# Attention and a mixture of experts on one core: 76 transfers a sequence in place of 103, with two experts' units interleaved on the partitions

## The chip, the core and the metric

The kernel runs on one core of one Trainium2 chip. The core has four compute engines: TensorE (PE, matrix products into PSUM banks), VectorE (DVE), ScalarE (ACT) and GpSimd (POOL). Each works through its own list of instructions in order and waits on semaphores for the others. A fifth, SyncE (SP), issues the transfers (DMAs); each raises a semaphore by 16 when it has landed. The metric is the device time of one execution in microseconds (us). Lower is better.

## What is computed

Sixteen sequences of 512 tokens with 128 channels pass one transformer layer in float32: causal attention with 16 heads of 64, a residual with layer norm, and a mixture of 32 experts of which 8 are chosen for each token.

```python
# attention, on h = layernorm(x)
q, k, v = (einsum('bsd,hde->bhse', h, W) for W in (Wq, Wk, Wv))
attn = softmax(where(causal, q @ k.T / sqrt(64), -inf))
y = h + concat_heads(attn @ v) @ Wo
x1 = x + layernorm(y, eps=1e-3) * gamma + beta
# experts, on h2 = layernorm(x1)
probs = softmax(h2 @ gate_w.T)                  # 32 experts
comb = top-8 of probs, divided by their sum, 0 elsewhere
for e in range(32):
    g, u = split(h2 @ gate_up_w[e].T)           # 64 each
    out += ((u * silu(g)) @ down_w[e].T) * comb[:, e]
result = x1 + out
```

## The kernel before

Everything of a sequence stays in SBUF. Products are made in float16 parts (`product`: high x high, high x low, low x high), so most tiles exist as a high half, written by ACT, and a low half, written by DVE or POOL. The four engines and SP have their orders written out by hand. The attention of sequence n, the experts of sequence n-1 (its last units, n-2) and the first steps of sequence n+1 are interleaved; a loop `for n in range(2, B - 2)` repeats one such list, and the first two and the last two sequences have lists of their own.

*Scores.* Projections give keys and queries of a pair of heads in `nat`. `place_qk(m, q)` (lines 303 to 312) copies them with six transfers, three for each head, 1 MB in all, to one of five slots of `score_ops`. The largest score of each row is found by DVE in a first, rough pass; POOL (`split_maxima`) scales it and splits it into high and low, PE turns it (`turn_maxima`), ACT copies the result to `rowmaxT` (`copy_maxima`), of 32 rows with 128 columns for a quad of four heads. `place_max(m, g)` (lines 314 to 321) puts these rows into two partitions of QB, so that the product subtracts them. Rows 16k to 16k+15 belong to pair k of the quad, eight for its high parts and eight for its low ones; there is one transfer for each eight. `scores` (line 457 on) waits for `placed[pair]` and, for each first head of a quad, for `max_placed`. ACT then takes exponentials (`exps`, L848) and the high half (`p_high`), POOL the low half (`p_low`, L1497), and PE multiplies by the values (`times_v`).

*Experts.* DVE makes the weights `comb` of 128 tokens x 4 chunks x 32 experts (`weigh`, L1210), PE turns them (`turn_weights`, L535), ACT copies them to `combT`, and `keep_weights(p)` (line 323) stores them as rows of the DRAM tensor `comb_rows`, one for an expert, with one transfer for each chunk. A unit j is a pair of experts, 64 partitions for each; `spread_weights(p, j)` (line 329, issues L335) reads its two rows of weights back and copies each to 64 partitions of `weighed(p, j)`, one of a ring of four buffers (`RING`), which is free when `unit_low(p, j-4)` is done. POOL multiplies the unit by it (`weigh_unit`, L1512), ACT takes the high half (`unit_high`), POOL the low half (`unit_low`, L1516), and PE multiplies by the down weights (`down_product`). In the last sequence each unit has a buffer of its own and DVE does the multiplication (`weigh_last`).

SP's list in the loop, with the order that matters below: 

```python
place_max(n, 3)
spread_weights(n - 1, 4); place_qk(n + 1, 0); spread_weights(n - 1, 5); spread_weights(n - 1, 6)
spread_weights(n - 1, 7); load_xb(n); place_qk(n + 1, 1); spread_weights(n - 1, 8)
spread_weights(n - 1, 9); place_qk(n + 1, 2); place_max(n + 1, 0); spread_weights(n - 1, 10)
```

PE's list in the loop comes to `scores(n + 1, 0, 0)`, which needs that `place_max(n + 1, 0)`, after `up_product(n - 1, 9)` and the projections of pair 3, and to `times_v(n + 1, 0)` some ten microseconds behind. A sequence has 103 transfers: 48 of keys and queries, 16 of maxima, 4 stores and 32 spreads of weights, two loads of x and one store of the result.

Of the kernel before, what the change touches and what calls it, by code (L numbers as in the profile page):

```python
# [53 lines left out]
def layer(nc, x, wq, wk, wv, wo, gamma, beta, gate, gate_up, down, ident_c, mask_c,  # L54
          key_rows_c, query_rows_c, tail_c, out):
    with ExitStack() as ctx:
# [14 lines left out]
        def slot_of(m, q):  # L71
# [60 lines left out]
        a_hi, a_lo = halves[:, 0], halves[:, 1]  # L132
        logits, dropped, shifted, ex, comb = (
            sb(name, [P, C, NE], F32) for name in ("logits", "dropped", "shifted", "ex", "comb"))
        top8 = sb("top8", [P, C, TOPK], F32)
# [140 lines left out]
        def _(sp):  # L276
# [37 lines left out]
            def place_max(m, g):  # L314
                wait(sp, score_mm, UNITS * 2 * (m * PAIRS + 2 * g + 1 - SLOTS + 1))
                sp.wait_ge(rowmaxT_ready, m * QUADS + g + 1)
                for k in range(2):
                    home = QB[E:E + MAX_ROWS, slot_of(m, 2 * g + k)].rearrange("a b (c p) -> a (b c) p", c=C)
                    for part in range(2):
                        at = 16 * k + 8 * part  # L320
                        sp.dma_start(home[part:part + 1], rowmaxT[at:at + 8, :]).then_inc(max_placed[g], 16)  # L321

            def keep_weights(p):
                sp.wait_ge(combT_ready, p + 1)
                wait(sp, a32_done, p * EP)
                for c in range(C):
                    sp.dma_start(comb_rows[:, c * P:c * P + P], combT[c * NE:c * NE + NE, :]).then_inc(comb_stored, 16)

            def spread_weights(p, j):
                if j == 0:  # L330
                    sp.wait_ge(comb_stored, 16 * C * (p + 1))
                if p < B - 1:
                    wait(sp, a_lo_done, p * EP + j - RING + 1)
                for e in range(2):
                    sp.dma_start(weighed(p, j)[ED * e:ED * e + ED, :],  # L335
                                 comb_rows[2 * j + e:2 * j + e + 1, :].to_broadcast([ED, S])).then_inc(spread_sem(p, j), 16)

# [49 lines left out]
        def _(pe):  # L387
# [73 lines left out]
            def scores(m, h, u):  # L461
                pair, ab, b = h // 2, h % 2, score_bank(h, u)
                slot = slot_of(m, pair)
                take(b, exp_done, m * H * UNITS + h * UNITS + u + 1)
                if m == 0 and h == 0 and u == 0:
                    pe.wait_ge(rows_loaded, 80)
                    pe.wait_ge(rows_filled, 4)
                if u == 0 and ab == 0:
                    pe.wait_ge(placed[pair], 96 * (m + 1))
                    if h % 4 == 0:  # L470
                        pe.wait_ge(max_placed[h // 4], 64 * (m + 1))
                for t in ((0,), (1, 3), (2,))[u]:
                    cols, at = S - t * P, (384 if t == 3 else 0)
                    dst = bank[b][:, at:at + cols]
                    keys = slice(t * P, t * P + P)
                    mm(dst, KA[:, slot, ab, keys], QA[:, slot, ab, t * P:S], True, False, True)
                    if t == 0:
                        mm(dst[:, P - 4:P], tail[:, 0:P], tail[:, P:P + 4], False, False, True)
                    n = BARRED_BY[t]
                    for side, first, end in ((KB0, 2 * n, cols), (KB1, 0, n), (KB2, n, 2 * n)):  # L480
                        last = mm(dst[:, first:end], side[:, slot, ab, keys], QB[:, slot, ab, t * P + first:t * P + end], False, True, True)
                last.then_inc(score_mm, 1)
# [49 lines left out]
            def turn_weights(m):  # L532
                take(XB, combT_ready, m + 1)
                pe.wait_ge(comb_done, m + 1)
                pe.transpose(bank[XB][:, 0:P], comb[:, :, :].rearrange("p c e -> p (c e)"), ident32[:, :]).then_inc(combT_mm, 1)  # L535

# [247 lines left out]
        def _(act):  # L784
# [53 lines left out]
            def copy_maxima(m, g, b):  # L838
                act.wait_ge(rowmaxT_mm, m * QUADS + g + 1)
                wait(act, max_placed[(g - 1) % QUADS], 64 * (m + 1) if g else 64 * m)  # L840
                copy(rowmaxT[:, :], bank[b][0:8 * C, 0:P]).then_inc(rowmaxT_ready, 1)
# [185 lines left out]
        def _(dve):  # L1027
# [170 lines left out]
            def weigh(p):  # L1198
# [10 lines left out]
                wait(dve, combT_mm, p)  # L1209
                dve.tensor_tensor(comb[:, :, :], exm[:, :, :], exinv[:, :].rearrange("p (c a) -> p c a", a=1).to_broadcast([P, C, NE]),  # L1210
                                  ALU.mult).then_inc(comb_done, 1)
# [15 lines left out]
            def weigh_last(p, j):  # L1227
                dve.wait_ge(su_done, p * EP + j + 1)
                dve.wait_ge(last_spread[j], 32)
                dve.tensor_tensor(weighed(p, j), weighed(p, j), unit(p, j), ALU.mult).then_inc(last_weighed, 1)  # L1230
# [232 lines left out]
        def _(pool):  # L1463
# [45 lines left out]
            def weigh_unit(p, j):  # L1509
                pool.wait_ge(su_done, p * EP + j + 1)  # L1510
                pool.wait_ge(comb_spread[j % RING], 32 * (p * (EP // RING) + j // RING + 1))
                pool.tensor_tensor(weighed(p, j), weighed(p, j), unit(p, j), ALU.mult).then_inc(a32_done, 1)  # L1512
# [119 lines left out]
```

## Time and profile before

| | |
|---|---|
| three timed runs, median | 1753.68 us |
| lowest, highest | 1750.7, 1754.48 us |
| the profiled execution, its own time | 1747.59 us |
| its span, first to last instruction | 1745.7 us |
| mean granted TensorE clock in it | 0.991 of full |
| busy: PE, DVE, ACT, POOL | 1633.9, 1462.4, 1404.4, 1403.9 us |

In the rows of the profile, L389 is the line of the helper that issues all ordinary matrix products, and L786 that of the helper for ACT's copies, so operations are told apart by the tiles that they write and read. SPq stands for SP's queue: the time of a row there is that of issuing transfers, not of moving data. A row of the timeline gives start, duration, engine, line, operation, output and inputs, and how many were merged (x4); brackets give the idle time ahead of it and what ended that. Everything is in microseconds, and times of the timeline count from the span's start.

### The profile page before, as it was taken

What the parts mean: (1) busy time and instruction counts of PE and PEld (TensorE: products, weight loads), DVE (VectorE), ACT (ScalarE), POOL (GpSimd) and SP (SyncE); (2) the same over time, 40 slices, a digit from 0 to 9 for tenths busy, and PEclk for the clock granted to TensorE, in tenths of its full rate; (3) what the DMA queues carried; (4) which work ended last, traced back from release to release, by engine and by line L of the source; (5) the groups of instructions that cost most, each with busy time, mean ns of one, the idle gap of its engine ahead of it and who ended that gap; (6) DMA issues with size and microseconds to landing.
All of it is one profiled execution on the core that took longest, in us unless ns stands there. A gap on an engine that the chain in (4) does not pass through costs nothing.

```text
span 1745.7 us, 56980 instructions
## 1 busy us (share of the span) xinstructions
PE 1633.9 (94%) x21209; PEld 1113.7 (64%) x21209; DVE 1462.4 (84%) x4484; ACT 1404.4 (80%) x2364; POOL 1403.9 (80%) x1164
## 2 busy tenths in 40 slices
PE   3799999999999999999999999999999999999868
PEld 1366766666666666666666666666676666667655
DVE  7999889797887978879797887979889797887757
ACT  2799888797887879788797888879788787888752
POOL 4477997888879788887888979788897888889880
PEclk9999999999999999999999999999999999999999
DMA  5554554646455464544646454473645546435423
GB/s 181 128 122 106 145 136 123 166 106 158 104 132 129 106 178 110 142 115 115 174 106 159 110 140 124 104 186 95 158 117 133 139 106 165 123 109 138 112 79 105
DMA packets 219444, 226.26 MB, mean 130 GB/s; under 512 B 27041, under 2 KB 185249, under 8 KB 218913
## 3 DMA queue, kind: packets, MB, share of 16 engines
q1 hardware_dynamic: 219168, 222.61, 49.8%
q8 instruction: 170, 2.79, 0.7%
q14 instruction: 106, 0.86, 0.2%
HBM read 82.53 MB, written 5.24 MB: 50 GB/s over the span
## 4 chain that ended last, share of the span: by engine, by line
PE 61%; SPq 8%; DVE 8%; DMA 6%; POOL 6%; issue 5%; ACT 5%; POOLq 0%; ACTq 0%; DVEq 0%
PE bank_r L389 15%; PE bank_s L389 12%; PE bank_v L389 8%; PE bank_g L389 8%; PE bank_u L389 8%; PE bank_x L389 7%; SPq L321 3%; POOL p_lo L1497 2%; DMA expert_room<-comb_rows 2%; SPq L335 2%; SPq L311 1%; SPq L312 1%; POOL expert_room L1512 1%; DMA xt<-in_x 1%; SPq L310 1%
## 5 line engine op out<-in xcount | busy, mean ns | idle before, releaser
L1497 POOL TENSOR_TENSOR p_lo<-p,p_hi 128x1280 f16<-128x1280 f32 x256 | 674.7, 2636 | 149.0 <-ACT p_hi L786 148.2
L848 ACT ACTIVATE p<-bank_s,back 128x512 f32<-128x512 f32 (+1 forms) x768 | 461.4, 615 | 61.9 <-PE bank_s L389 53.8
L389 PE MATMUL bank_s<-score_ops 128*128 128x62 f16 (+10 forms) x4096 | 405.6, 233 | 20.6 <-DMA score_ops<-rowmaxT 15.3
L389 PEld LDWEIGHTS bank_s<-score_ops 128*128 128x128 f16 x4096 | 278.1, 97 | 192.5 <-issue 46.8
L1512 POOL TENSOR_TENSOR expert_room<-expert_room 128x512 f32<-128x512 f32 x240 | 304.4, 1275 | 34.7 <-DMA expert_room<-comb_rows 17.4
L786 ACT ACTIVATE p_hi<-p 128x1280 f16<-128x1280 f32 x256 | 324.6, 1268 | 7.8 <-PE bank_r L389 2.2
L1516 POOL TENSOR_TENSOR halves<-expert_room,halves 128x512 f16<-128x512 f32 x240 | 276.4, 1162 | 29.0 <-ACT halves L786 27.3
L1124 DVE CUSTOM_DVE_ANT_0 max_junk<-bank_r,mask 128x384 f16<-128x384 f32 (+3 forms) x523 | 232.1, 474 | 36.6 <-PE bank_g L389 16.3
L389 PE MATMUL bank_x<-w_hi,halves 128*128 128x128 f16 x1920 | 199.1, 220 | 2.0 <-POOL halves L1516 2.0
L786 ACT ACTIVATE halves<-expert_room 128x512 f16<-128x512 f32 x240 | 150.1, 625 | 44.8 <-POOL expert_room L1512 32.2
L389 PE MATMUL bank_x<-w_lo,halves 128*128 128x128 f16 x960 | 173.2, 220 | 0.0
L389 PEld LDWEIGHTS bank_x<-w_hi,halves 128*128 128x128 f16 x1920 | 155.2, 98 | 20.3 <-issue 6.2
L389 PE MATMUL bank_r<-nat 64*128 64x384 f16 (+3 forms) x523 | 106.1, 300 | 15.3 <-DVE o L1137 9.8
L1124 DVE CUSTOM_DVE_ANT_0 max_junk<-bank_u,mask 128x512 f16<-128x512 f32 (+3 forms) x202 | 99.0, 505 | 6.1 <-PE bank_g L389 4.0
L389 PE MATMUL bank_r<-tanh_room,w_hi 128*128 128x512 f16 x338 | 101.8, 383 | 0.5 <-DVE o L1137 0.4
L389 PEld LDWEIGHTS bank_x<-w_lo,halves 128*128 128x128 f16 x960 | 94.1, 98 | 7.3
L389 PE MATMUL bank_r<-v_hi,p_hi 128*128 128x65 f16 x870 | 87.9, 194 | 2.1 <-POOL p_lo L1497 1.4
L389 PE MATMUL bank_r<-v_hi,p_lo 128*128 128x65 f16 x870 | 87.9, 194 | 0.0
L389 PE MATMUL bank_r<-v_lo,p_hi 128*128 128x64 f16 x870 | 87.8, 192 | 0.0
L786 ACT ACTIVATE nat<-bank_r 128x512 f16<-128x512 f32 x110 | 65.9, 599 | 26.2 <-PE bank_r L389 24.1
L389 PE MATMUL bank_u<-tanh_room,w_hi 128*128 128x512 f16 x264 | 78.7, 380 | 7.5 <-DVE v_lo L1112 6.2
L1124 DVE DVE_READ_ACCUMULATOR2_ANT rowmax<- 128x1 f32 x1024 | 85.2, 83 | 0.1
(298 smaller groups left out, 5015.4 us busy)
## 6 DMA issues: line engine op xcount, KB each, us to landing
score_ops<-nat SPq DMA_DIRECT2D x256, 256.0 KB, 3.8
score_ops<-nat SPq DMA_DIRECT2D x512, 128.0 KB, 3.6
expert_room<-comb_rows SPq DMA_DIRECT2D x480, 128.0 KB, 3.0
xt<-in_x SPq DMA_DIRECT2D x16, 256.0 KB, 3.5
xb<-in_x SPq DMA_DIRECT2D x16, 256.0 KB, 4.1
score_ops<-rowmaxT SPq DMA_DIRECT2D x256, 2.0 KB
out_y<-expert_room SPq DMA_DIRECT2D x16, 256.0 KB, 3.4
score_ops<-comb_rows SPq DMA_DIRECT2D x32, 128.0 KB, 3.0
```

Source lines behind the costliest of these rows:

```text
L310: sp.dma_start(score_ops[0:E, 0:4, slot, ab, :], home[rows, K_HI:K_HI + 1].to_broadcast([E, 4, S])).then_inc(placed[q], 16)
L311: sp.dma_start(score_ops[0:E, 4:6, slot, ab, :], home[rows, Q_HI:Q_LO + 1]).then_inc(placed[q], 16)
L312: sp.dma_start(score_ops[E:P, 0:5:4, slot, ab, :], home[rows, K_LO:Q_HI + 1]).then_inc(placed[q], 16)
L321: sp.dma_start(home[part:part + 1], rowmaxT[at:at + 8, :]).then_inc(max_placed[g], 16)
L335: sp.dma_start(weighed(p, j)[ED * e:ED * e + ED, :], comb_rows[2 * j + e:2 * j + e + 1, :].to_broadcast([ED, S])).then_inc(spread_sem(p, j ...
L389: return pe.matmul(dst, lhsT, rhs, start=start, stop=stop, skip_group_check=shared)
L786: return act.activation(dst, src, ACT.Copy)
L848: act.activation(p32[:, h % P_SLOTS, at:at + cols], bank[score_bank(h, u)][:, 0:cols], ACT.Exp, scale=back[:, SC_SCORE:SC_SCORE + 1]).then ...
L1124: done = dve.tensor_tensor_reduce(max_junk[:, k % 2, at:at + cols], bank[b][:, at:at + cols], mask[:, S - cols:S], 1.0, NEG, ALU.add, ALU. ...
L1497: pool.tensor_tensor(p_lo[:, slot, :], p32[:, slot, :], p_hi[:, slot, :], ALU.subtract).then_inc(p_lo_done, 1)
L1512: pool.tensor_tensor(weighed(p, j), weighed(p, j), unit(p, j), ALU.mult).then_inc(a32_done, 1)
L1516: pool.tensor_tensor(a_lo[:, j % 2, :], weighed(p, j), a_hi[:, j % 2, :], ALU.subtract).then_inc(a_lo_done, 1)
```

## The change

Three kinds of transfer are merged, and the lists of all engines and their order stay.

- `place_max` issues one transfer for each pair of heads (16 rows to two partitions) in place of two (8 rows to one partition): 8 a sequence for 16.
- `keep_weights` issues one store for four. So that the rows of `combT` come out in the order of `comb_rows`, `comb` is laid out with the expert ahead of the chunk; DVE writes it through a rearranged view.
- `spread_weights` issues one transfer of 256 KB for two of 128 KB: 16 a sequence for 32. Its 128 partitions read two rows in turn, so even partitions hold the first expert of the unit and odd ones the second. The gate, up and down weights are interleaved on the host in the same way.

The counts in the waits on `max_placed`, `comb_stored` and the spreads' semaphores are halved or quartered to match. The number of bytes moved is the same.

```diff
-            sb(name, [P, C, NE], F32) for name in ("logits", "dropped", "shifted", "ex", "comb"))
+            sb(name, [P, C, NE], F32) for name in ("logits", "dropped", "shifted", "ex"))
+        comb = sb("comb", [P, NE, C], F32)
...
-                    for part in range(2):
-                        at = 16 * k + 8 * part
-                        sp.dma_start(home[part:part + 1], rowmaxT[at:at + 8, :]).then_inc(max_placed[g], 16)
+                    sp.dma_start(home, rowmaxT[16 * k:16 * k + 16, :]).then_inc(max_placed[g], 16)
...
-                for c in range(C):
-                    sp.dma_start(comb_rows[:, c * P:c * P + P], combT[c * NE:c * NE + NE, :]).then_inc(comb_stored, 16)
+                sp.dma_start(comb_rows.rearrange("e (c p) -> (e c) p", c=C), combT).then_inc(comb_stored, 16)
...
-                    sp.wait_ge(comb_stored, 16 * C * (p + 1))
+                    sp.wait_ge(comb_stored, 16 * (p + 1))
...
-                for e in range(2):
-                    sp.dma_start(weighed(p, j)[ED * e:ED * e + ED, :],
-                                 comb_rows[2 * j + e:2 * j + e + 1, :].to_broadcast([ED, S])).then_inc(spread_sem(p, j), 16)
+                sp.dma_start(weighed(p, j),
+                             comb_rows[2 * j:2 * j + 2].rearrange("a (b s) -> b a s", b=1).to_broadcast([ED, 2, S])).then_inc(spread_sem(p, j), 16)
...
-                        pe.wait_ge(max_placed[h // 4], 64 * (m + 1))
+                        pe.wait_ge(max_placed[h // 4], 32 * (m + 1))
...
-                pe.transpose(bank[XB][:, 0:P], comb[:, :, :].rearrange("p c e -> p (c e)"), ident32[:, :]).then_inc(combT_mm, 1)
+                pe.transpose(bank[XB][:, 0:P], comb[:, :, :].rearrange("p e c -> p (e c)"), ident32[:, :]).then_inc(combT_mm, 1)
...
-                dve.tensor_tensor(comb[:, :, :], exm[:, :, :], exinv[:, :].rearrange("p (c a) -> p c a", a=1).to_broadcast([P, C, NE]),
+                dve.tensor_tensor(comb[:, :, :].rearrange("p e c -> p c e"), exm[:, :, :], exinv[:, :].rearrange("p (c a) -> p c a", a=1).to_broadcast([P, C, NE]),
                                   ALU.mult).then_inc(comb_done, 1)
...
-    gu = gate_up_w.reshape(EP, 2, 2, ED, D).transpose(4, 0, 2, 1, 3)
+    gu = gate_up_w.reshape(EP, 2, 2, ED, D).transpose(4, 0, 2, 3, 1)
...
-        "down": cont(down_w.reshape(EP, 2, D, ED).transpose(1, 3, 0, 2).reshape(P, EP * D)),
+        "down": cont(down_w.reshape(EP, 2, D, ED).transpose(3, 1, 0, 2).reshape(P, EP * D)),
```

## Rows read from the trace of the kernel before

**Rows 1.** The page: span, busy time of PE, and packets of the DMA engines.

```profile
span 1745.7 us, 56980 instructions
PE 1633.9 (94%) x21209; PEld 1113.7 (64%) x21209; DVE 1462.4 (84%) x4484; ACT 1404.4 (80%) x2364; POOL 1403.9 (80%) x1164
DMA packets 219444, 226.26 MB, mean 130 GB/s; under 512 B 27041, under 2 KB 185249, under 8 KB 218913
```

**Rows 2.** Busy time by stretches: the sum of eight stretches of 103.3 us, 332.0 to 1157.7.

```profile
sum 826.40, PE 798.97 PEld 548.03 DVE 701.32 ACT 693.71 POOL 700.78; mean PE 99.87 PEld 68.50 DVE 87.67 ACT 86.71 POOL 87.60
```

**Rows 3.** List of waits, whole run: who waited, for whom, us, times, longest.

```profile
PE bank_s L389 <- DMA score_ops<-rowmaxT: 15.3, 13, 2.2
PE bank_r L389 <- DVE o L1137: 10.2, 13, 0.9
PE bank_x L535 <- DVE comb L1210: 4.4, 12, 0.4
PE bank_u L389 <- POOL p_lo L1497: 2.8, 2, 2.3
PE bank_x L389 <- POOL halves L1516: 2.0, 6, 0.8
...
POOL p_lo L1497 <- ACT p_hi L786: 148.2, 95, 3.5
...
POOL expert_room L1512 <- DMA expert_room<-comb_rows: 17.4, 16, 2.7
```

**Rows 4.** Chain of waits, 905 to 951.5: start, us, what.

```profile
930.40 4.13 DMA expert_room<-comb_rows
...
949.31 1.68 DMA score_ops<-rowmaxT
```

**Rows 5.** Timeline of ACT and of PE around 951.

```profile
943.52 0.27 ACT L786 ACTIVATE rowmaxT<-bank_v 32x128 f16<-32x128 f32 x1 [1.39 <-PE bank_v L389]
...
951.12 0.38 PE L389 MATMUL bank_s<-score_ops 128*128 128x512 f16 x1 [1.15 <-DMA score_ops<-rowmaxT]
```

**Rows 6.** Timeline of SP's issues, 920.5 to 952.

```profile
921.09 2.79 SPq L321 DMA_DIRECT2D score_ops<-rowmaxT  x4
...
929.75 4.60 SPq L335 DMA_DIRECT2D expert_room<-comb_rows  x6
...
942.10 0.63 SPq L310 DMA_DIRECT2D score_ops<-nat  x1
...
946.45 0.61 SPq L312 DMA_DIRECT2D score_ops<-nat  x1
947.15 2.79 SPq L321 DMA_DIRECT2D score_ops<-rowmaxT  x4
```

**Rows 7.** Issues by line (ns: shortest/median/longest), and time from issue to landing.

```profile
L335 SPq DMA_DIRECT2D expert_room<-comb_rows x480: 444/597/1612, 173.5 to 1683.6; - x160
DMA to landing us min/median/max: 2.7/3.0/5.5
...
L321 SPq DMA_DIRECT2D score_ops<-rowmaxT x256: 634/653/872, 53.7 to 1644.6; - x128
...
score_ops<-nat SPq DMA_DIRECT2D x256, 256.0 KB, 3.8
```

**Rows 8.** Timeline of POOL, 930 to 957.

```profile
929.04 1.17 POOL L1516 TENSOR_TENSOR halves<-expert_room,halves 128x512 f16<-128x512 f32 x1
930.76 2.62 POOL L1497 TENSOR_TENSOR p_lo<-p,p_hi 128x1280 f16<-128x1280 f32 x1 [0.56 <-ACT p_hi L786]
934.67 1.27 POOL L1512 TENSOR_TENSOR expert_room<-expert_room 128x512 f32<-128x512 f32 x1 [1.28 <-DMA expert_room<-comb_rows]
```

**Rows 9.** Busy time by stretches; last: PE's clock, DMA engines' share, GB/s.

```profile
939.40:947.10 7.70, 7.41 (x104) 5.48 (x105) 6.49 (x21) 5.44 (x10) 7.47 (x8) 1.00 1.01 230
```

**Rows 10.** The tile comb, 905 to 912: ns of its multiplication.

```profile
L1210 DVE TENSOR_TENSOR comb<-bank_x,exinv x1: 291/291/291, 905.8 to 905.8; 128x128 f32<-128x128 f32 x1
```

**Rows 11.** Timeline of PE at the same step of the next sequence.

```profile
1054.02 0.38 PE L389 MATMUL bank_s<-score_ops 128*128 128x512 f16 x1 [0.33 <-DMA score_ops<-rowmaxT]
```

More of the change, by code:

```diff
@@ L132, in layer @@
         a_hi, a_lo = halves[:, 0], halves[:, 1]
-        logits, dropped, shifted, ex, comb = (
-            sb(name, [P, C, NE], F32) for name in ("logits", "dropped", "shifted", "ex", "comb"))
+        logits, dropped, shifted, ex = (
+            sb(name, [P, C, NE], F32) for name in ("logits", "dropped", "shifted", "ex"))
+        comb = sb("comb", [P, NE, C], F32)
         top8 = sb("top8", [P, C, TOPK], F32)
@@ L839, in copy_maxima @@
                 act.wait_ge(rowmaxT_mm, m * QUADS + g + 1)
-                wait(act, max_placed[(g - 1) % QUADS], 64 * (m + 1) if g else 64 * m)
+                wait(act, max_placed[(g - 1) % QUADS], 32 * (m + 1) if g else 32 * m)
                 copy(rowmaxT[:, :], bank[b][0:8 * C, 0:P]).then_inc(rowmaxT_ready, 1)
@@ L1228, in weigh_last @@
                 dve.wait_ge(su_done, p * EP + j + 1)
-                dve.wait_ge(last_spread[j], 32)
+                dve.wait_ge(last_spread[j], 16)
                 dve.tensor_tensor(weighed(p, j), weighed(p, j), unit(p, j), ALU.mult).then_inc(last_weighed, 1)
@@ L1510, in weigh_unit @@
                 pool.wait_ge(su_done, p * EP + j + 1)
-                pool.wait_ge(comb_spread[j % RING], 32 * (p * (EP // RING) + j // RING + 1))
+                pool.wait_ge(comb_spread[j % RING], 16 * (p * (EP // RING) + j // RING + 1))
                 pool.tensor_tensor(weighed(p, j), weighed(p, j), unit(p, j), ALU.mult).then_inc(a32_done, 1)
```

## The prediction

> **What bounds the kernel now.** I read the page's busy shares first. PE is busy 94% of the span [rows 1]: PE sets the pace, and what can be won is its idle time. Cut into eight sequences of 103.3 us, the run shows PE busy 99.87 us in each [rows 2], so 3.4 us are idle. The list of waits says for what. PE's largest entry is the landing of the row maxima, 15.3 us in 13 waits, about one of 1.2 us in each looped sequence; the next of the loop is 10.2 us for DVE's o, which the change doesn't touch [rows 3]. POOL has 17.4 us in 16 waits for spread weights [rows 3].
>
> Why do the maxima land late? In the chain of waits the last thing before 951.0 us is their landing, 1.68 us from issue [rows 4], and PE, idle for 1.15 us, then starts the first score product of the next sequence [rows 5]. So the wait is for `place_max(n+1, 0)`. Its data were ready long before: ACT's copy to rowmaxT ended at 943.79 [rows 5]. What it waits for is the queue: on SP the last issue of `place_qk(n+1, 2)` ends at 947.06 and the maxima begin at 947.15 [rows 6].
>
> **The stretch replayed with the change.** SP pays about the same for every issue: 0.60 us for a spread of 128 KB, 0.65 for a maximum of 2 KB [rows 7], with 0.04 to 0.1 between two. I take these for the merged forms; the bounds are 0.44 and 1.61, the shortest and longest spread [rows 7]. I start at 921.09, which hangs on ACT's copy for quad 3 and so stays, and follow the list of SP.
> - From 921.09 to 929.75 SP issues four maxima (2.79 us), two halves of spread 4 and the six transfers of `place_qk(n+1, 0)` [rows 6]. Two maxima and one half fall away, 2 x 0.70 + 0.69 = 2.1 us, so spread 5 is issued at 927.6 and not in halves at 929.75 and 930.4.
> - The second half landed 4.13 us after its issue, at 934.53 [rows 4], and POOL, free since 933.38, waited 1.28 us for it [rows 8]. Merged it may take 3.0 us (the median of 128 KB) or 6.0 (twice that); nat's transfer, 256 KB too, has 3.8 [rows 7]. I take 4.1, near to the half's own 4.13 at this place: 931.7. POOL's wait is gone, with 1.7 us to spare; at 6.0 it would be 0.2.
> - Spread 6 ends at 928.8. Spread 7 needs `unit_low` 3, whose subtraction ends at 930.21 [rows 8]: here SP really waits, and is through at 930.9. xb follows (0.6), then `place_qk(n+1, 1)` with the 4.3 that the first took (the 8.66 us above less maxima and spread): 935.8. Spreads 8 and 9 need the next two subtractions, which POOL now reaches 1.28 us earlier, the second at 936.9: SP is through at 937.5. `place_qk(n+1, 2)` takes its 5.0 us (942.10 to 947.06 [rows 6]): 942.5.
> - `place_max(n+1, 0)` is then held by ACT's copy (943.79) and not by the queue: two issues, at 943.9 and 944.6, for four from 947.15.
>
> The landing: no row has sixteen rows of 256 B going to two partitions. It can't be sooner than a single part now, 1.68 us [rows 4]; above stands the nat transfer of 256 KB, 3.8 us [rows 7]. So it lands between 946.3 and 948.4, and PE asks for it at 949.97 [rows 5]: hidden at both ends, by 3.7 or 1.6 us. I take 1.7, since the data are those of the first row.
>
> How the rows are spread over engines is what a rule speaks against. The page counts 27041 packets under 512 B [rows 1]. If each of the 1648 transfers of the sixteen sequences ended in sixteen small packets that would be 26368, and the 2048 rows of maxima on top make 28416, too many by 1375; with eight for a maximum it is 26368 in all, and the first loads fill the rest. The Trainium skill, page "DMA: Bandwidth & Descriptors", section "Why a DMA increments its semaphore by 16 and not by 1", gives the reason: a transfer runs on the largest number of engines up to 16 that divides the slowest dimension of both sides. By that rule the trace's eight are right, a merged maximum (two partitions at the destination) runs on two engines with eight rows each, and the section "Rules for kernel authors" of the same page advises to keep all sixteen in use. The sum by that rule is the same: the maximum lands somewhere within the bounds above.
>
> Bandwidth could hold the queue too. From 939.4 to 947.1 the DMA engines are full, share 1.01 at 230 GB/s [rows 9]. The bytes don't change. Three `place_qk` of 1 MB, five spreads and xb of 256 KB are 4.7 million bytes, 20.5 us at 230 GB/s; begun at 923.3 (925.4 before) that ends at 943.8, again no later than ACT's copy. The engines allow it, just.
>
> **The sum**, against the profiled run: span 1745.7 us [rows 1], its own time 1747.6; the median of the three timed runs is 1753.7, 6.1 more.
> - PE's 13 waits for the maxima [rows 3], all removed: -15.3.
> - POOL's waits for spreads [rows 3] fall, but POOL is not the bound. PE waits 2.0 us for its halves and 2.8 for p_lo [rows 3], so 0 to -4.8; I take -1, since what POOL itself waits for is mostly ACT's p_hi, 148.2 us [rows 3].
> - The maxima of the other three quads, `place_qk` and the loads of x come earlier, and PE's list has no wait for any of them: 0. Their cover is PE's work on the heads before.
> - `keep_weights`, one issue for four, lands 1 to 1.5 us sooner; POOL's first weighed unit follows, inside the 17.4 us above: 0.
> - `comb` with experts outermost: DVE stores with a stride. It takes 0.29 us now [rows 10], and PE waits for it 4.4 us in 12 waits [rows 3]. A gain is excluded (as many elements, strided). At most I let it double: 0.29 x 16 = +4.6. I take 0, its own row. Weights are reordered on the host and their products keep their shapes: 0.
> - Given back: PE, 1.2 us early, meets what was next latest. In the sequence that ends at 1054 PE came late by itself, and the wait was only 0.33 us [rows 11]: the wait absorbs delays that would show otherwise. Bounds 0 and +7 (0.5 us in each of 14 sequences); I take 15% of the gain, +2.3, since POOL and SP advance at the same time.
> - The fill and the last sequence: no wait of PE for a DMA stands in the list there: 0. For the last, each spread has a buffer of its own.
>
> Together -15.3 - 1 + 2.3 = -14.0 us. Profiled 1733.6; in the median 1753.7 - 14.1 = 1739.6.
>
> **Rivals.**
> *Half of it.* The maxima are early, but PE meets ACT or POOL almost at once; 7 us stay, 1746.7. For it speaks the 0.33 us above; against, that POOL, too, loses its 1.28 us wait ahead of this place.
> *Nothing.* The change doesn't shorten the queue: a merged issue costs SP as much as its two parts, as there are as many rows to describe, and the maxima come when they come now. 1753.7. Against it: 2 KB and 128 KB cost nearly the same issue [rows 7].
> *More.* SP leaves the loop's chain altogether, and PE wins 1 us more of its remaining 2.2 us a sequence, in 13: 1726.
> *Slower.* The merged spread lands so late that the ring of four starves POOL. The places: spread 5 (issued 927.6, needed 933.4, 5.8 us) and spread 10, which follows `unit_low` 6 at about 949 and is weighed near 955.3, 6.2 us. It decides from a landing of 6 us, twice the 3.0 of a half. At 8 us POOL waits 2.2 + 1.8 us a sequence for 1.3 now, 2.7 more; less PE's 1.2 that is +1.5 x 13 = +20: 1773.7. Against it: no half took over 5.5 us [rows 7].
>
> **How the numbers follow.** Forecast (1732 to 1745) 0.55, more 0.10, half 0.15, nothing 0.12, slower 0.08. The predicted time is the forecast's, 1739.6. The range, 1726 to 1754, reaches from "more" to "nothing"; the slower case and the far ends are left out. Under 0.2% (3.5 us) a change can't be told from none here. Faster: forecast, more and nearly all of half, 0.78; same: nothing, with a little of half, 0.13; slower 0.09.
>
> **What the changed profile would show.** PE's entry for the DMA of rowmaxT gone, or under 2 us; POOL's for spreads under 6; SP waiting longer for ACT's rowmaxT and POOL's halves, as these now start its work; 128 maxima issues at 0.65 us, spreads at 0.60 and landing in 3.4 to 4.1; a sequence of 102.3 us. The prediction is wrong if merged issues take over 0.9 us, if PE's 15 us come back under ACT p or POOL p_lo, or if spreads land after 6 us.

## The result, and the profile after

The changed kernel takes 1711.3 us (median of four runs, 1710.19 to 1712.3) against 1752.19 for the kernel before (four runs, 1746.62 to 1754.48): 0.9771 of it, with a 95% interval of 0.9746 to 0.9796, 41 us less. In the profiled executions the span fell from 1745.7 to 1710.5 us, by 35.2.

The page after, its first lines, the packets, the shares of the chain that ended last, and one row of its DMA issues (instructions, KB each, median us from issue to landing):

```profile
span 1710.5 us, 56548 instructions
PE 1626.2 (95%) x21209; PEld 1111.5 (65%) x21209; DVE 1463.2 (86%) x4484; ACT 1400.7 (82%) x2364; POOL 1402.4 (82%) x1164
...
DMA packets 212783, 226.20 MB, mean 132 GB/s; under 512 B 20384, under 2 KB 178592, under 8 KB 212256
...
PE 82%; DVE 8%; POOL 4%; issue 4%; ACT 1%; DMA 0%; SPq 0%; POOLq 0%; DVEq 0%; ACTq 0%
...
expert_room<-comb_rows SPq DMA_DIRECT2D x240, 256.0 KB, 3.5
```

Before, the same line of the chain began with these shares:

```profile
PE 61%; SPq 8%; DVE 8%; DMA 6%; POOL 6%; issue 5%; ACT 5%; POOLq 0%; ACTq 0%; DVEq 0%
```

SP's queue and the DMAs, together 14% of the chain, are gone from it. PE's waits after (for whom, us, times, longest) have no entry for the maxima, where [rows 3] had 15.3 us in 13; of the two waits of the first row one is in the fill (11.8 us), the other behind the loop:

```profile
PE bank_r L386 <- DVE hT L1099: 13.0, 2, 11.8
PE bank_r L386 <- DVE o L1134: 10.0, 13, 0.9
...
PE bank_x L532 <- DVE comb L1207: 6.0, 13, 0.5
```

SP, on the other hand, waits more for its data. Its waits, before and then after:

```profile
SPq L307 <- DVE nat L1107: 180.7, 46, 20.5
SPq L316 <- ACT rowmaxT L786: 144.3, 34, 7.8
SPq L335 <- POOL halves L1516: 109.8, 72, 5.7
```

```profile
SPq L308 <- DVE nat L1104: 240.9, 60, 21.0
SPq L317 <- ACT rowmaxT L783: 211.2, 44, 10.1
SPq L332 <- POOL halves L1513: 205.2, 116, 8.0
```

**Where the time went.** PE turns `comb` once in each sequence, so two such rows tell how long a sequence takes. Timeline of PE before, one row a sequence:

```profile
906.22 0.30 PE L535 MATMUL bank_x<-ident,comb 128*128 128x128 f32 x1 [0.37 <-DVE comb L1210]
1009.55 0.30 PE L535 MATMUL bank_x<-ident,comb 128*128 128x128 f32 x1 [0.37 <-DVE comb L1210]
1113.94 0.30 PE L535 MATMUL bank_x<-ident,comb 128*128 128x128 f32 x1 [0.37 <-DVE comb L1210]
```

and after (481.34 and 582.68 are neighbours, and 278.67 and 1393.86 eleven sequences apart):

```profile
278.67 0.30 PE L532 MATMUL bank_x<-ident,comb 128*128 128x128 f32 x1 [0.46 <-DVE comb L1207]
481.34 0.30 PE L532 MATMUL bank_x<-ident,comb 128*128 128x128 f32 x1 [0.46 <-DVE comb L1207]
582.68 0.30 PE L532 MATMUL bank_x<-ident,comb 128*128 128x128 f32 x1 [0.47 <-DVE comb L1207]
...
1393.86 0.30 PE L532 MATMUL bank_x<-ident,comb 128*128 128x128 f32 x1 [0.46 <-DVE comb L1207]
```

Before, these sequences take 103.3 and 104.4 us; over ten of the loop, each measured from one PE instruction to the same one a sequence later, 102.8 to 106.9, 104.2 on average. After, they take 101.3 to 101.6: (1393.86 - 278.67) / 11 = 101.4. The ten give 28.4 of the 35.2 us, the sequences behind them and the tail 7.4; the fill ahead is 0.5 longer. I call that time of a sequence its period below.

### The profile page after: what moved, and what is told of

Same layout as the page of the kernel before. It is cut to its first block, busy times and chain, and to the rows that moved or that the text cites. A ratio compares the mean times of both kernels' runs of the same rounds, so it can differ in the third digit from the quotient of the medians.

```text
span 1710.5 us, 56548 instructions
## 1 busy us (share of the span) xinstructions
PE 1626.2 (95%) x21209; PEld 1111.5 (65%) x21209; DVE 1463.2 (86%) x4484; ACT 1400.7 (82%) x2364; POOL 1402.4 (82%) x1164
## 4 chain that ended last, share of the span: by engine, by line
PE 82%; DVE 8%; POOL 4%; issue 4%; ACT 1%; DMA 0%; SPq 0%; POOLq 0%; DVEq 0%; ACTq 0%
PE bank_r L386 20%; PE bank_s L386 15%; PE bank_v L386 11%; PE bank_u L386 11%; PE bank_g L386 10%; PE bank_x L386 10%; POOL p_lo L1494 2%; PE bank_r L395 2%; DVE max_junk L1121 1%; PE bank_v L395 1%; DVE stats L1028 1%; PE bank_x L395 1%; POOL halves L1513 1%; POOL expert_room L1509 1%; DVE x L1160 1%
## 5 line engine op out<-in xcount | busy, mean ns | idle before, releaser
L386 PE MATMUL bank_r<-tanh_room,w_hi 128*128 128x512 f16 x338 | 101.7, 383 | 0.5 <-DVE o L1134 0.4
L386 PEld LDWEIGHTS bank_r<-v_hi,p_hi 128*128 128x128 f16 x870 | 79.1, 98 | 6.1 <-issue 2.1
```

What stands on the lines that cost most here:

```text
L386: return pe.matmul(dst, lhsT, rhs, start=start, stop=stop, skip_group_check=shared)
```

## The experiments

Each kernel was timed beside the kernel before on the same chip; those medians were 1748.12 us (e1 to e4), 1749.9 (e5, e6, e10 and e11) and 1750.41 (the two e9, e12 and e14). The two e9 kernels have two runs each, the others four to ten. The table holds what each gave; "period" is the mean of ten looped sequences in the profiled execution, and the last two columns are PE's waits for the maxima and DVE's for x, in us over the run.

| kernel | us | ratio, 95% interval | period | maxima | x |
|---|---|---|---|---|---|
| before (profiled) | | 1 | 104.2 | 15.3 | 21.2 |
| after | 1711.3 | 0.9771, 0.9746 to 0.9796 | 101.4 | none | 2.8 |
| e1_maxima | 1710.17 | 0.9775, 0.9754 to 0.9796 | 101.5 | 1.5 | 3.7 |
| e2_spreads | 1726.32 | 0.9875, 0.9849 to 0.9902 | 102.3 | 8.7 | 9.8 |
| e3_store | 1749.94 | 1.0005, 0.9986 to 1.0025 | 104.4 | 21.4 | 18.7 |
| e4_padded | 1735.12 | 0.9924, 0.9901 to 0.9947 | 103.4 | 11.3 | 17.2 |
| e5_load_first | 1744.29 | 0.9972, 0.9955 to 0.9989 | 103.9 | 21.3 | 3.0 |
| e6_quad0 | 1730.23 | 0.9908, 0.9883 to 0.9934 | 102.9 | 5.7 | 21.1 |
| e10_quad0_load | 1726.51 | 0.9883, 0.9863 to 0.9903 | 102.6 | 7.5 | 2.8 |
| e11_padded_full | 1773.61 | 1.0171, 1.0132 to 1.021 | 105.9 | 23.7 | 27.9 |
| e9_late5 | 1710.81 | 0.9776, 0.9747 to 0.9805 | 101.5 | 1.0 | 3.0 |
| e9_late14 | 1794.98 | 1.0257, 1.0226 to 1.0288 | 108.4 | 53.5 | 2.9 |
| e12_no_store | 1709.13 | 0.9767, 0.9747 to 0.9787 | 101.4 | none | 2.7 |
| e14_no_store_stats_later | 1710.15 | 0.9772, 0.9753 to 0.9792 | 101.4 | none | 2.7 |

### Which of the three parts brings the gain

Each part alone, on the kernel before; the cuts (`...`) are the counts in the waits and what else goes with the part. The maxima:

```diff
-                    for part in range(2):
-                        at = 16 * k + 8 * part
-                        sp.dma_start(home[part:part + 1], rowmaxT[at:at + 8, :]).then_inc(max_placed[g], 16)
+                    sp.dma_start(home, rowmaxT[16 * k:16 * k + 16, :]).then_inc(max_placed[g], 16)
...
```

> The kernel before with the merged maxima alone (8 issues a sequence fewer, 95 transfers). Theory A (the 15.3 us of PE waits for the maxima were the limit, and each microsecond taken from the queue just ahead of place_max(n+1, 0) comes off them): 1.4 us fewer at this place than the 1.2 us that PE waits, so PE's entry for the DMA of rowmaxT falls below 3 us, and with what hangs on it the time is 1752 - 15 to - 22, about 1734. Theory B (SP's issue time in sum sets the pace, wherever it is saved): 8 of the 27 issues, 0.3 x 40 = 12 us, about 1740. Theory C (the maxima matter only together with an earlier spread): under 4 us, 1749.

The spreads, with the weights interleaved on the host:

```diff
-                for e in range(2):
-                    sp.dma_start(weighed(p, j)[ED * e:ED * e + ED, :],
-                                 comb_rows[2 * j + e:2 * j + e + 1, :].to_broadcast([ED, S])).then_inc(spread_sem(p, j), 16)
+                sp.dma_start(weighed(p, j),
+                             comb_rows[2 * j:2 * j + 2].rearrange("a (b s) -> b a s", b=1).to_broadcast([ED, 2, S])).then_inc(spread_sem(p, j), 16)
...
```

> The kernel before with the merged spreads alone (16 issues fewer, weights interleaved on the host). The maxima stand as before, four issues, but six spread issues fewer lie between quad 3's maxima and quad 0's of the next sequence, 3.9 us. Theory A: the wait for the maxima goes here too, and the wait of DVE for x shrinks (one issue fewer ahead of the load), so 1752 - 25 to - 35, about 1722. Theory B (issue time in sum): 16 of 27, -24, 1728. Landing theory (256 KB lands later than two halves did, and eats it): above 1745, with POOL's wait for spreads over 17 us.

The store, with the other layout of `comb`:

```diff
-                for c in range(C):
-                    sp.dma_start(comb_rows[:, c * P:c * P + P], combT[c * NE:c * NE + NE, :]).then_inc(comb_stored, 16)
+                sp.dma_start(comb_rows.rearrange("e (c p) -> (e c) p", c=C), combT).then_inc(comb_stored, 16)
...
```

> The kernel before with the merged store alone and comb laid out with the expert first (3 issues fewer). DVE's strided multiplication took 0.384 us in the changed kernel for 0.291 before, and PE's wait for it 6.0 us for 4.4. Theory A: SP has slack after the store, so nothing is won at the maxima 40 us later, and PE pays 1.6 us more: 1752 to 1754. Theory B (issue time in sum): 3 of 27, -4, 1748.

Eight merged maxima of the 27 transfers saved give all of it: 1710.17 us, far below the lowest of the three figures written ahead (about 1734). The spreads alone give 22 us, the store alone nothing that can be told from none. Waits of `e1_maxima`, then of `e2_spreads`:

```profile
PE bank_s L387 <- DMA score_ops<-rowmaxT: 1.5, 3, 0.7
```

```profile
PE bank_s L388 <- DMA score_ops<-rowmaxT: 8.7, 8, 2.6
...
SPq L334 <- POOL halves L1515: 178.6, 105, 7.8
```

22 + 38 is far more than 41: the parts don't add up, they run against a common floor, a period of 101.4 us. And 16 spreads saved are 16 x 0.69 = 11 us of SP's time in a sequence but win only 1.9 of period, while 8 maxima, 5.6 us of SP's time, win 2.7. I read it so: what counts is which issues lie between SP's last real wait and the issue that PE is waiting for. `unit_low` holds spread 7 at 930.2 in the replayed stretch, and what the halves ahead of it save turns into waiting: SP's wait for `halves` is 178.6 us in `e2_spreads` for 109.8 before.

### Is it SP's time, or something else about the merged transfers?

The changed kernel with 27 small transfers of 0.5 KB a sequence put back on SP, one where each removed one was; nothing waits for them but their own buffers.

```diff
+                for _ in range(count):
...
+                    wait(sp, pad_sem[k], 16 * (n // PADS))
+                    sp.dma_start(pads[:, k, :], ident_c[0:16, 0:16]).then_inc(pad_sem[k], 16)
...
+                    padding(1)
                     sp.dma_start(home, rowmaxT[16 * k:16 * k + 16, :]).then_inc(max_placed[g], 16)
...
+                padding(3)
                 sp.dma_start(comb_rows.rearrange("e (c p) -> (e c) p", c=C), combT).then_inc(comb_stored, 16)
...
+                padding(1)
                 sp.dma_start(weighed(p, j),
...
```

> The changed kernel with 27 small transfers a sequence (16 rows of 32 bytes from DRAM to a buffer that nothing reads) put back on SP's queue where the merging took one away: one ahead of each maximum, three ahead of the store, one ahead of each spread. If SP's issue time is the cause, the time comes back to that of the kernel before, 1748 to 1756, with 15 us of PE waits for the maxima. If it is the merged transfers' landing, their packets or the DMA engines' load, it stays near 1711.

Their issue took 0.418 us (median), less than the removed ones, so 27 x 0.418 = 11.3 us came back of 16 x 0.60 + 8 x 0.65 + 3 x 0.42 = 16.1. With that, two thirds of the gain are gone (a ratio of 0.9924 for 0.9771), between the two outcomes that were written ahead, and the waits have come back: 11.3 us for the maxima and 17.2 for x. To pay the whole price the small transfers were then made like a maximum, 8 rows of 256 B from SBUF to SBUF:

```diff
-                    sp.dma_start(pads[:, k, :], ident_c[0:16, 0:16]).then_inc(pad_sem[k], 16)
+                    sp.dma_start(pads[:, k, :], ident[0:8, :]).then_inc(pad_sem[k], 16)
...
```

> The changed kernel with 27 dummy transfers a sequence as in e4_padded, but each like a maximum (8 rows of 256 bytes, SBUF to SBUF). In e4_padded a dummy's issue was 0.42 us for the 0.65 that was removed, so 11.3 of 17.7 us of SP's time came back, and 25 of 41 us of the gain. If issue time on SP is all, dummies of 0.65 bring the whole back: 1746 to 1753. If a part belongs to the merged transfers themselves (one landing for two), the time stays at 1735 to 1740.

Their row of issues (ns min, median, max; first and last start), and the kernel's waits:

```profile
L305 SPq DMA_DIRECT2D pads<-ident x432: 624/669/1502, 54.9 to 1758.7; - x144
```

```profile
PE bank_s L405 <- DMA score_ops<-rowmaxT: 23.7, 14, 3.0
...
PE bank_u L405 <- DVE v_lo L1128: 10.1, 11, 2.5
```

27 x 0.669 = 18.1 us a sequence, 2.0 more than was taken out, and the kernel is slower than before by 1.7%, beyond the 1746 to 1753 us written ahead, with a period 1.6 us longer than before's (105.85 for 104.22). The merged transfers, with their two engines, their interleaved partitions and their 256 KB, are all still in it. So nothing in the merged form itself brings the gain; SP's time does. What stays open is whether the small transfers cost something beyond their issue: they are packets too, and POOL's wait for spreads is 28.3 us here for 17.4 before. SP was not held up in any run without a transfer.

### Where in SP's list it counts

The trace of before has two of PE's waits behind SP. One is for the maxima. The other is hidden: `load_x(n + 2)` stands behind a `place_max` and a spread, DVE's `stats` wait for it, `v_lo` behind them on DVE is late, and PE waits for `v_lo`. Before, the load issued at 765.73 made DVE wait and then PE (waits of 766 to 775, then PE's timeline):

```profile
DVE stats L1031 <- DMA xt<-in_x: 2.5, 1, 2.5
```

```profile
772.35 0.61 PE L389 MATMUL bank_u<-tanh_room,w_hi 128*128 128x512 f16 x2 [1.36 <-DVE v_lo L1112]
```

Over the run DVE waits 21.2 us in 13 for x, PE 6.2 us in 5 for `v_lo` at this bank (7.6 at all four). The two places were mended apart. In `e5_load_first` the load is issued ahead of the maxima of quad 1:

```diff
-                place_max(n, 1); spread_weights(n - 2, 15); load_x(n + 2); place_qk(n, 5); place_max(n, 2)
+                load_x(n + 2); place_max(n, 1); spread_weights(n - 2, 15); place_qk(n, 5); place_max(n, 2)
```

> The kernel before with one step moved in SP's loop: load_x(n+2) is issued ahead of place_max(n, 1) and spread 15 and not behind them, six issues earlier (about 4 us). No transfer is merged. In the kernel before DVE waited 21.2 us in 13 waits for x, and PE 6.2 us in 5 waits for the v_lo that DVE makes behind it; with merged maxima both are nearly gone. If this is a second path of the gain, DVE's wait for x goes and PE's for v_lo with it: -6 to -8, 1742. If the wait for v_lo only moves into the wait for the maxima (PE comes there 1 us earlier and waits 1 us longer, as SP's queue sets the pace), the time stays: 1748 to 1751, with PE's entry for the maxima at 20 us or more.

In `e6_quad0` the maxima are merged for the first quad only, two issues saved of 103:

```diff
+                    if g == 0:
+                        sp.dma_start(home, rowmaxT[16 * k:16 * k + 16, :]).then_inc(max_placed[g], 16)
+                        continue
...
```

> The kernel before with merged maxima for quad 0 alone, 2 issues a sequence fewer, 1.4 us just ahead of the wait of PE. Theory A (the wait itself, 15.3 us, and the 1.2 us a time that it is long): -15 to -18, 1732; the remaining 20 us of the gain of all merged maxima come from quads 1 to 3, above all quad 1's that stand ahead of the load of x, and quad 3's that stand 26 us ahead in the same full stretch of the queue. Theory A2 (this place alone gives the whole gain, since SP's loop is the period and one link less in it frees everything): -35, 1712. If SP's time in sum counted evenly: 2/27 of 40, -3.

and `e10_quad0_load` has both edits.

> Both edits: quad 0's maxima merged and load_x ahead of quad 1's. If two paths add, the time is that of quad 0 alone less 6 to 8 us; if the load only showed because SP's queue was the pace, it gives nothing alone and 6 to 8 here. With all merged maxima the time was 1710; this should come to 1720 to 1726, the rest being quad 3's issues.

PE's waits for the maxima in `e5_load_first`, then PE's waits in `e6_quad0`:

```profile
PE bank_s L389 <- DMA score_ops<-rowmaxT: 21.3, 18, 2.8
```

```profile
PE bank_u L392 <- DVE v_lo L1115: 5.8, 6, 1.4
PE bank_s L392 <- DMA score_ops<-rowmaxT: 5.7, 10, 1.2
```

With the load first, PE's wait for `v_lo` at bank_u is gone and the wait for the maxima is 6.0 us longer than in the profile of before, as if PE arrived there sooner, at a queue that is no sooner ready. That size proves little, though: `e3_store`, no faster than before, lists 21.4 us in 17 for the maxima. The time falls by only 5.6 us.

With two issues less ahead of the first product, 20 us are won, close to the case in which the wait itself is all (1732) and far from the one in which this place alone brings the whole gain (1712); the period is 102.9 for 104.2, 1.3 us for the 1.4 us that two issues take. In the profiled executions the span fell by 15.9 us (1745.7 to 1729.8) and the *listed* wait for the maxima by only 9.6. Here is the error of my sum in one experiment: the gain was larger than the wait that went away. Other entries went with it: ACT's p, 4.2 to 0.8 us, and o, 10.2 to 8.2. Both edits together give 23 us, 3.7 more than `e6_quad0` alone, where 6 to 8 more were expected.

### How much room the changed kernel has, and what lateness costs

Small transfers just ahead of `place_max(n + 1, 0)` in the changed kernel, 5 in one and 14 in the other:

```diff
-                spread_weights(n - 1, 9); place_qk(n + 1, 2); place_max(n + 1, 0); spread_weights(n - 1, 10)
+                spread_weights(n - 1, 9); place_qk(n + 1, 2); padding(5); place_max(n + 1, 0); spread_weights(n - 1, 10)
```

> The changed kernel with five small dummy transfers a sequence just ahead of place_max(n+1, 0), 0.42 + 0.05 us each on SP, 2.3 us in all. In the changed kernel SP is through with place_qk(n+1, 2) 0.8 us ahead of ACT's copy, and the maxima land about 3.6 us before PE asks. If PE's own work is now the limit with that slack, nothing happens: 1708 to 1714, a sequence stays at 101.3 us. If SP's time still counts, 14 x 2.3 = +32.

> The same with fourteen dummies, 6.6 us, 2.2 us more than the slack of 4.4. Theory (slack first, then one for one): 2.2 us in each of 12 loop sequences, +26, and each PE stall of 2 us or more followed by 3.4 us at half of TensorE's clock, 1.7 us, where the kernel before had three of those: 1737 to 1760. If the wait costs what it lists and no more: 1737 with no drop of the granted clock. If the queue recovers in other places: under 1725.

Five cost nothing (1710.81 us, a wait of 1.0 us in 2, with 5 x 0.42 = 2.1 us of issues ahead): some 2 us of room are there, as the replay said. Fourteen gave 1794.98 us, far outside the 1737 to 1760 written ahead. First, they take SP 8.65 us in the profiled execution and not 6.6: SP also waits for the buffers of its own small transfers, 9.7 us in 9 over the run. With the 4.3 us of room that the changed kernel shows (0.8 ahead of ACT's copy, 3.5 behind the landing, next section) that leaves 4.4 for PE to wait. Second, the clock. PE's wait in `e9_late14` over the run, and three stretches of one sequence (length, busy us of PE, PEld, DVE, ACT and POOL with instructions, granted clock, DMA share, GB/s):

```profile
PE bank_s L401 <- DMA score_ops<-rowmaxT: 53.5, 12, 5.5
```

```profile
860.00:865.30 5.30, 1.28 (x6) 0.39 (x4) 2.17 (x7) 1.90 (x3) 4.69 (x3) 0.89 0.03 2
865.30:868.70 3.40, 2.86 (x17) 1.41 (x18) 1.24 (x4) 0.96 (x2) 0.00 (x0) 0.50 0.69 205
868.70:872.10 3.40, 3.40 (x29) 2.43 (x28) 1.54 (x5) 1.76 (x4) 1.34 (x2) 0.67 0.88 208
```

A wait is 53.5 / 12 = 4.5 us, but the period grew by 7.0 us, from 101.4 to 108.4. Behind the wait the granted clock is 0.50 while PE is busy for 2.86 us (1.2 and not 2.4 GHz) and 0.67 in the next 3.4: 1.4 + 1.1 = 2.5 us of lost PE time in this sequence. Over ten sequences PE's busy time is 102.3 us each for 99.9 in the changed kernel, 2.4 more, and 4.5 + 2.4 = 6.9 is about the 7.0 seen.

### Is more to be had?

`e12_no_store` is the changed kernel with the store and the layout of `comb` put back as before; the maxima and the spreads stay merged.

```diff
-                sp.dma_start(comb_rows.rearrange("e (c p) -> (e c) p", c=C), combT).then_inc(comb_stored, 16)
+                for c in range(C):
+                    sp.dma_start(comb_rows[:, c * P:c * P + P], combT[c * NE:c * NE + NE, :]).then_inc(comb_stored, 16)
...
```

> The changed kernel without the merged store: comb stays with the chunk first, four stores. DVE's multiplication goes from 0.384 back to 0.291 us and PE's wait for comb from 6.0 to 4.4 us; SP has slack where the three issues stand. Theory (PE is the limit, at 101.3 us a sequence): -1.6, 1709.7. If the store's issues matter: up to +2.

It gave 1709.13 us, 2 less than the changed kernel; the intervals of the two ratios (0.9747 to 0.9787, 0.9746 to 0.9796) overlap, so it may be the better one and wasn't shown to be. Its wait for `comb` is 4.8 us where after has 6.0.

The largest wait of the loop that is left is for DVE's o, 10.0 us in 13. `e14_no_store_stats_later` is `e12_no_store` with the layer norm's statistics on DVE moved behind the division that makes o:

```diff
-                row_maximum(n, 6, 1, 1, V); add_input(n - 1); second_stats(n - 1); h_low(n + 1, R1); divide(n, 5, G)
+                row_maximum(n, 6, 1, 1, V); add_input(n - 1); h_low(n + 1, R1); divide(n, 5, G); second_stats(n - 1)
```

> As e12_no_store, and one step of DVE's loop moved: h_low(n+1) and divide(n, 5) go ahead of second_stats(n-1) and not behind it. PE's largest wait of the loop in the changed kernel is 0.79 us for that o, 10.0 us in 13 waits. If it is what is next on PE's path, 0.5 to 0.8 us come off each of 12 sequences, -6 to -9: 1702. If the second layer norm, 1.2 us later, is waited for in its place (PE for y, ACT for the shift): 1708 to 1715.

PE's entry for o falls from 10.0 us to 0.4, and the period is still 101.4. Following PE's instructions one by one against `e12_no_store`, 8.7 us are won at the place over ten sequences. Of these 5.9 are lost again at two of the next seven products, scores for which PE now waits for ACT's p, and the rest within some fifty products; the PE entries for ACT's p are, in `e12_no_store` and then in this kernel:

```profile
PE bank_s L386 <- ACT p L845: 0.6, 3, 0.2
```

```profile
PE bank_s L386 <- ACT p L845: 3.4, 16, 0.2
```

So here too the listed wait was not what could be won. What sets the floor of 101.4 us was not isolated further: PE is busy 99.94 us of it.

## Why the prediction was wrong

The direction and the cause were right, the size wasn't: -14 us forecast, -35.2 in the span, and 1711.3 us lies below the range's 1726. Point by point.

**What bounds the kernel: right.** PE waited for the queue and not for data. `e11_padded_full` shows it: the merged transfers stay, SP's time is given back, and the gain is gone.

**The replay: right to under 1 us up to the maxima.** SP's timeline after, of the same stretch (`place_qk`'s last issue, then the maxima), ACT's copy, and PE's first score product:

```profile
922.15 0.73 SPq L313 DMA_DIRECT2D score_ops<-nat  x1
923.72 1.39 SPq L320 DMA_DIRECT2D score_ops<-rowmaxT  x2
```

```profile
923.38 0.27 ACT L783 ACTIVATE rowmaxT<-bank_v 32x128 f16<-32x128 f32 x1 [1.40 <-PE bank_v L386]
```

```profile
929.67 0.38 PE L386 MATMUL bank_s<-score_ops 128*128 128x512 f16 x1
```

The queue is free at 922.88, ACT's copy ends at 923.65, and the maxima go out at 923.72: held by the copy, with two issues for four, as forecast. The landing of such a merged maximum stands in the chain of `e9_late14` (start, us):

```profile
863.96 1.74 DMA score_ops<-rowmaxT
```

With 1.74 us from the second issue, at about 924.4, it has landed at 926.2, and PE asks for it at 929.67, 3.5 us later (forecast 3.7 to 1.6 us).

**The prices of merged forms: right for the issues, and for the landing in the median alone.** Issues after, in ns (min, median, max), the landing of the spreads in us, and one multiplication of POOL in the replayed stretch:

```profile
L332 SPq DMA_DIRECT2D expert_room<-comb_rows x240: 512/576/1432, 171.8 to 1647.5; - x120
DMA to landing us min/median/max: 2.8/3.6/10.3
```

```profile
L320 SPq DMA_DIRECT2D score_ops<-rowmaxT x128: 637/675/782, 55.0 to 1607.3; - x128
```

```profile
914.31 1.27 POOL L1509 TENSOR_TENSOR expert_room<-expert_room 128x512 f32<-128x512 f32 x1 [0.45 <-DMA expert_room<-comb_rows]
```

0.576 and 0.675 us against 0.60 and 0.65 taken; spreads land after 3.5 us (3.6 with the last sequence's), between the 3.0 of a half and the 4.1 I took. But their landing spreads: none of the halves took over 5.5 us, and of 240 merged ones in `expert_room` 16 took over 6 and 4 over 8, the longest 10.3. In the replayed stretch the spread issued at 908.9 took 5.3 us and not 4.1, POOL waited 0.45 us for it where the replay had 1.7 to spare, and the two issued at 917.2 and 917.8 took 6.7 and 7.3 and were not waited for. Over the run POOL's wait for spreads fell all the same, from 17.4 to 1.3 us. The store was put at 0 and is (`e3_store`, 1.0005). `comb` takes 0.384 us for 0.291, and PE waits 1.6 us more for it (6.0 for 4.4): inside the bounds of 0 and +4.6.

**The step that failed: the wait as the measure of the gain.** The sum took 15.3 us away, since that is what PE's list shows for the maxima, gave 2.3 back, and put at 0 all else that hangs on SP but POOL's 1. The gain was 35.2. A listed wait is only the part of the queue's delay that PE hasn't already been delayed by elsewhere. Each sequence took as long as a chain through SP took: SP waits for `nat` and for row maxima, which PE and DVE make late because SP was late a sequence earlier, and PE's lateness was spread over many small waits besides the one for the maxima. This account of the loop is read from SP's waits and from the 14% that SP's queue and the DMAs had of the chain; what the runs show is the price. `e6_quad0` measures it: 1.4 us of SP's time taken off ahead of the maxima shortens the period by 1.3. It ends where PE's own 101.4 is reached, so there were 104.2 - 101.4 = 2.8 us a sequence to be won. Most of that could have been had from the profile of before: over ten real sequences PE is busy 1008.4 us (first row; the second is of the changed kernel, and the columns are those above).

```profile
278.08:1320.30 1042.22, 1008.40 (x13291) 691.85 (x13291) 883.93 (x2761) 876.28 (x1481) 886.51 (x741) 1.00 0.52 131
```

```profile
278.67:1292.51 1013.84, 999.40 (x13290) 689.58 (x13291) 884.73 (x2761) 873.62 (x1481) 885.80 (x741) 1.00 0.54 135
```

That is 100.8 us a sequence. With 0.3 off for the two stretches at half clock in it, and the waits that the change leaves alone, o's 0.8 and `comb`'s 0.4, the floor comes to 101.7, 2.5 of the 2.8 us. This is "more", the rival of 1726, taken further; it had 0.10.

Smaller misses add to it.
- *The period.* I took the eight stretches of 103.3 us [rows 2] for sequences; 103.3 was the distance between two of them. The mean of ten is 104.2, and single ones are 102.8 to 106.9. So 99.87 us was PE's busy time in less than a sequence. The idle time of 3.4 us a sequence came out right by luck (1042.2 - 1008.4 is 33.8 in ten): both its terms were 0.9 to 1.0 too small.
- *The loads of x at 0.* "PE's list has no wait for any of them" held for PE's own entries, but DVE waited 21.2 us for x, and PE 7.6 us for `v_lo` behind it. After, x is waited for 2.8 us and `v_lo` 0.9. `e5_load_first` shows the link; it also shows that this wait alone was worth only 5.6 us.
- *The clock, not in the sum.* In the profiled execution of before the granted clock is 0.50 for 3.4 us at three places behind the fill. Two come right behind waits for the maxima, of 2.25 us (ended 426.99) and 1.92 (741.31; the rows are in the last section). The third, at 1520.4, follows two waits for DVE of 1.14 and 0.55 us; `e1_maxima` and `e12_no_store` have one near this step as well, so its absence in the changed kernel can't be put down to the merged maxima. Each costs 1.7 us. The changed kernel has none in its loop. Its four runs have mean granted clocks of 0.990 to 0.993 and lie within 2.1 us, where the nine runs of before beside the last four kernels have 0.984 to 0.992 and lie between 1745 and 1753.5.
- *The give-back had the wrong sign.* PE's idle time fell by 27.5 us (1745.7 - 1633.9 = 111.8, to 84.3), more than the entry of 15.3. Besides the maxima -15.3 it is `v_lo` -6.7, ACT's p -3.6, and POOL's p_lo and `halves` -3.0 where I had -1; against them `comb` +1.6. PE's busy time fell by 7.7: by 9.0 in the ten sequences, of which the clock is 3.4 and 5.6 is unexplained, and by 1.7 behind them, while it rose by 3.0 in the fill, where the changed kernel has 13.6 us at half clock for 6.8. 27.5 + 7.7 = 35.2.

The medians moved by 40.9 us and the spans of the profiled executions by 35.2: the execution of before that was profiled is one of its fastest (1747.59 of 1746.6 to 1754.5 us).

**The rivals.** "Nothing" hung on an issue that costs what its parts cost; it costs as much as one part. "Slower" hung on spreads landing after 6 us, and 8: that came up, in 16 and in 4 of 240, but not where POOL was short of time: its waits for spreads were 1.3 us in all. "Half" had PE meeting ACT or POOL at once; PE met nothing until 2.8 us further on. SP's waits rose as forecast.

**The rule on engines.** Packets under 512 B fell from 27041 to 25249 with the maxima alone, by 1792: 256 transfers on eight engines (2048) less 128 on two (256). With the spreads alone they fell by 4097, for 256 transfers less on sixteen. So the Trainium skill, page "DMA: Bandwidth & Descriptors", section "Why a DMA increments its semaphore by 16 and not by 1", is borne out to within one packet. Its advice to keep all sixteen in use (section "Rules for kernel authors") was worth nothing here: a maximum on two engines landed in 1.74 us, one on eight in 1.68, and going against it saved 0.65 us of issue each time.

## What to carry to other kernels

Where an in-order queue feeds the bounding engine in a loop, don't take the listed wait for the most that can be won: measure the period over many sequences, between the same instruction in each, compare it with the engine's busy time over the same stretch plus the waits that will stay, and start from that difference. Count issues and not bytes on SP, above all those between its last real wait and the one that is needed, and look one step behind: a transfer that only DVE waits for can be PE's wait two instructions later. The cheapest test is to add a few dummy transfers at the place: where the time rises by their issue time the queue is the bound, where it doesn't there is room.

## What the runs showed of the hardware

- **Issue time on SP hardly depends on the bytes.** 256 KB take 0.576 us, 128 KB 0.597 [rows 7], 2 KB from SBUF 0.65 to 0.67, 4 KB onto two partitions 0.675; a load of 0.5 KB from DRAM 0.418, the merged store of `comb` 0.344 (medians). All issues of before add up to 1093 us in its trace, 63% of the span, and that queue set the pace with its waits counted in. The Trainium skill, page "DMA: Bandwidth & Descriptors", section "Issuing engines are not separate DMA queues", calls the sequencer's time "usually small relative to the DMA itself"; here it is 0.60 of 3.0 us for half a spread and 0.65 of 1.7 for a maximum, which is over a third, and they add up on SP: the saving of eight such issues a sequence was the whole gain.
- **A strided write costs DVE a third more.** 128 elements a partition, float32, 0.291 us with a dense and 0.384 with a stride of 16 bytes, the same instruction otherwise.
- **A merged transfer can land much later than its parts did.** 256 KB to 128 partitions from two rows landed in 2.8 to 10.3 us, median 3.6; its halves of 128 KB in 2.7 to 5.5, median 3.0 [rows 7], and in `e1_maxima`, which is as fast as the changed kernel, in 2.6 to 5.1. With small transfers between them (`e4_padded`, `e11_padded_full`) the merged ones took at most 6.2 and 7.0.
- **A stall can cost more than its length.** Stretches of before around a wait of PE of 1.92 us that ended at 741.31 (columns as above):

```profile
739.00:741.30 2.30, 0.39 (x2) 0.02 (x1) 1.31 (x4) 1.54 (x2) 2.02 (x3) 1.00 0.05 13
741.30:742.20 0.90, 0.89 (x8) 0.44 (x8) 0.00 (x0) 0.23 (x1) 0.90 (x1) 1.00 0.29 112
742.20:743.40 1.20, 1.20 (x11) 0.74 (x10) 1.10 (x3) 0.59 (x2) 1.02 (x1) 0.50 0.58 198
743.40:745.60 2.20, 2.20 (x16) 1.52 (x15) 1.27 (x4) 1.13 (x2) 0.28 (x1) 0.50 0.82 230
745.60:750.00 4.40, 4.40 (x74) 3.46 (x73) 2.62 (x11) 2.99 (x5) 3.38 (x3) 1.00 0.81 198
```

The granted clock is 0.50 (1.2 GHz) for 3.4 us, a little after the products have begun again: 1.7 us lost on top of the 1.92. All twelve waits of `e9_late14`, of 3.8 to 5.5 us, have such a stretch beside them, of 3.4 or 6.8 us. It isn't every stall: in before, waits for the maxima of 1.55 us (ended 847.8) and 1.66 (1365.15), and one of 2.33 for p_lo (1631.08), have none behind them.
